# A decoder layer with a mixture of experts: the products into the experts as three f16 products, the expert's weights read in place, eight row buffers

## The chip, the cores and the metric

The kernel runs on one core of a Trainium2 chip. The metric is the device time of one execution in microseconds (us); lower is better. TensorE (PE) multiplies matrices, VectorE (DVE), ScalarE (ACT) and GpSimd (POOL) work elementwise, and SyncE (SP) issues transfers. "PEld" is the loading of a product's stationary operand (its weights) into PE; a "q" behind an engine's name means its sequencer, which runs register and issue instructions.

## The reference

One decoder layer over x, 128 batches of 64 rows of 128 numbers, thus 8192 tokens, or 64 tiles of 128. Three blocks follow each other, each added to its input and normalised: attention with retention ("ret"), attention over ctx_1024 ("cross"), and causal self attention ("self") with a mixture of 8 experts. The change touches the experts:

```python
probs = jax.nn.softmax(h @ wg, axis=-1)
topv, topi = jax.lax.top_k(probs, K)                 # K = 2 of E = 8
...
h1 = jax.nn.gelu(jnp.einsum('bsd,edf->ebsf', h, w1) + bb1[:, None, None, :])
y = jnp.einsum('ebsf,efd->ebsd', h1, w2) + bb2[:, None, None, :]
moe = jnp.einsum('ebsd,bse->bsd', y, w)
```

w1[e] is 128x512, w2[e] 512x128, all in float32.

## The kernel before, in words

**Attention.** The 192 tiles of the three blocks (64 each) go in 48 groups of four through a hand-written software pipeline. `sp_slot`, `pe_slot`, `act_slot`, `pool_slot` and `dve_slot` append to each engine's queue what it does in slot s, four slots to a group; every engine runs its queue in order and waits on semaphores. During the self groups a router picks two experts for each token, and POOL scatters the token's row (128 numbers, its number and its first choice) with an indirect DMA (L787) to `block_rows` in DRAM, a region for each expert.

**Weights.** `mixture` (L297) is a list of constants that SP loads one a slot in the cross phase, among them all experts' matrices and biases into one tile `wx` (L140), 1156 numbers an expert and partition: w1, w2, the 4 columns of bb1 and a row of bb2.

**The expert stage.** A block is 128 rows of one expert; there are NBLK = 135 of them. Which expert and which rows a block has is only known at run time: small tables `row_of` and `expert_of` are computed first for 73 early blocks and then, during the stage, for the rest. The loop at L1274 issues slot s: on SP `sp_expert` (L1181) reads a row number from the table into a register and loads `xrow` from `block_rows` at that address (L1188, L1189), at most four blocks ahead. DVE reads the expert's number (L1232) and copies its 1156 columns of `wx` to one of four buffers `we` (L1236). PE transposes the rows (L1194), ACT copies them to `hTb` (L1218). Four products of 128x128x128 (L1202) give the hidden layer, transposed, ACT adds bb1 and applies gelu (L1225), four products that accumulate (L1211) give the output, DVE adds bb2 (L1242), works out the row numbers (L1248), and POOL scatters 128 rows to `expert_rows` in DRAM (L1254). In slot s each engine takes the blocks in this order: out(s-3), transpose(s), in(s-1). Every third slot, for the first 54, also appends one slot of the tail of attention (`behind`). From slot 59 on, every fourth slot SP loads a piece of `x2b` (L1262).

The order on PE, which stays the same around the change (from L1274 on):

```python
if s >= 3:
    pe_expert_out(s - 3)
    dve_expert_out(s - 3)
...
if s < NBLK:
    sp_expert(s)
    pe_expert_turn(s)
    act_expert_turned(s)
if 1 <= s <= NBLK:
    pe_expert_in(s - 1)
    act_expert(s - 1)
```

A combine stage then weighs the two results of each token, normalises twice and stores.

## Time and profile before

| | us |
|---|---|
| median of 3 runs | 1290.16 |
| lowest, highest | 1288.4, 1293.84 |
| the profiled execution's own time | 1299.05 |
| its span | 1297.8 |
| first row load of the experts issued | 858.2 |
| last block's scatter issued | 1208.2 |

The mean granted clock of TensorE in the profiled execution is 0.893 of full speed. A page of the profile gives busy times over the whole span; views give the same for a stretch ("windows"), single instructions in order of time ("timeline"), all instructions of a source line with shortest, median and longest duration, who waited for whom ("waits"), and the chain of work that ended last.
### The profile page before, as it was taken

The numbers are of one execution on the slowest core, as the hardware profiler recorded it, in microseconds if no ns is written. First come the engines' busy times: TensorE is split into PE (matmuls) and PEld (weight loads), VectorE is DVE, ScalarE is ACT, GpSimd is POOL, SyncE is SP. The second block draws the span as 40 slices with busy tenths as digits, with TensorE's granted clock in tenths as the row PEclk, the third lists the DMA queues.
The fourth block names the chain that finished last, engine by engine and source line by source line (L and its number), as shares of the span: only waits on it lengthen the run. The fifth ranks groups of instructions, "written<-read, shape, count | busy, mean of one in ns | idle before, by whom it ended". The sixth has DMA issues, their size and how long they took to land.

```text
span 1297.8 us, 45997 instructions
## 1 busy us (share of the span) xinstructions
PE 1063.3 (82%) x17677; PEld 761.5 (59%) x17677; DVE 865.0 (67%) x2370; ACT 824.6 (64%) x1884; POOL 911.1 (70%) x859
## 2 busy tenths in 40 slices
PE   5888888788998888888988888847788799999552
PEld 2555555554555555555555555637777789999310
DVE  4677776766888777777767776545454466666485
ACT  2355554678999887777777776414445466666377
POOL 3788888866766657777777776766666656667596
PEclk9999898987999999989888997657889999999886
DMA  5465332221233223222222221111212233332453
GB/s 158 129 185 147 88 86 63 63 60 54 75 85 85 80 66 85 68 67 68 79 65 65 77 77 35 52 34 43 61 54 63 66 88 98 99 100 78 143 164 97
DMA packets 132181, 108.61 MB, mean 84 GB/s; under 512 B 19563, under 2 KB 122476, under 8 KB 131932
## 3 DMA queue, kind: packets, MB, share of 16 engines
q1 hardware_dynamic: 123548, 88.29, 24.9%
q0 software_dynamic: 8416, 17.38, 3.8%
q8 instruction: 141, 2.31, 0.8%
q14 instruction: 76, 0.62, 0.2%
HBM read 41.58 MB, written 26.75 MB: 53 GB/s over the span
## 4 chain that ended last, share of the span: by engine, by line
PE 42%; issue 14%; DVE 14%; POOL 14%; ACT 10%; DMA 3%; another core or an unknown queue 2%; DVEq 1%; SPq 1%; POOLq 0%; ACTq 0%
PE bank L1211 7%; PE bank L1202 7%; POOL Plo L769 7%; PE bank L547 3%; PE bank L612 3%; PE bank L550 3%; DVE P L841 2%; DMA xrow<-block_rows 2%; PE bank L487 2%; DVE st L873 2%; DVE mx L817 2%; PE bank L450 2%; PE bank L517 2%; PE bank L510 2%
## 5 line engine op out<-in xcount | busy, mean ns | idle before, releaser
L769 POOL TENSOR_TENSOR Plo<-P 128x1024 f16<-128x1024 f32 x192 | 364.7, 1901 | 162.2 <-ACT P L726 136.1
L1254 POOL DMA_INDIRECT expert_rows<-yo,ix x135 | 173.0, 1281 | 103.3 <-DVE ix L1248 73.4
L1225 ACT ACTIVATE G<-bank,we 128x128 f32<-128x128 f32 x540 | 154.9, 372 | 103.6 <-PE bank L1202 85.3
L817 DVE TENSOR_REDUCE mx<-bank 128x16 f16<-128x1024 f32 x128 | 156.7, 1225 | 42.3 <-PE bank L465 33.2
L687 ACT ACTIVATE Kz<-kh,col 128x512 f16<-128x512 f16 x256 | 167.1, 717 | 0.1
L1211 PE MATMUL bank<-we,G 128*128 128x128 f32 x1080 | 151.5, 286 | 16.7 <-ACT G L1225 12.6
L787 POOL DMA_INDIRECT block_rows<-xs,slots x128 | 132.6, 1036 | 39.8 <-issue 38.4
L510 PE MATMUL bank<-Vh,P 64*128 64x17 f16 (+1 forms) x3072 | 148.6, 170 | 10.2 <-issue 10.2
L726 ACT ACTIVATE P<-bank 128x1024 f32<-128x1024 f32 x128 | 131.1, 1024 | 39.7 <-PE bank L487 38.2
L510 PEld LDWEIGHTS bank<-Vh,P 64*128 64x128 bf16 x3072 | 125.6, 94 | 49.8 <-issue 37.2
L511 PE MATMUL bank<-Vh,Plo 64*128 64x17 f16 (+1 forms) x3072 | 145.9, 168 | 9.4 <-issue 9.3
L1202 PE MATMUL bank<-hTb,we 128*128 128x128 f32 x1080 | 149.1, 283 | 4.6 <-issue 4.4
L512 PE MATMUL bank<-Vl,P 64*128 64x16 f16 x3072 | 146.3, 167 | 7.4 <-issue 7.3
L1211 PEld LDWEIGHTS bank<-we,G 128*128 128x128 f32 x1080 | 138.1, 200 | 19.2 <-ACT G L1225 14.5
L1236 DVE COPY we<-wx 128x1156 f32 x135 | 104.4, 774 | 57.4 <-issue 54.1
L1202 PEld LDWEIGHTS bank<-hTb,we 128*128 128x128 f32 x1080 | 137.3, 199 | 5.6 <-issue 4.9
L512 PEld LDWEIGHTS bank<-Vl,P 64*128 64x128 bf16 x3072 | 127.4, 94 | 11.7 <-issue 11.6
L511 PEld LDWEIGHTS bank<-Vh,Plo 64*128 64x128 f16 x3072 | 127.9, 95 | 9.2 <-issue 9.2
L487 PEld LDWEIGHTS bank<-Qz,Kst 64*64 64x64 f16 x3072 | 60.8, 114 | 88.1 <-issue 62.1
L487 PE MATMUL bank<-Qz,Kst 64*64 64x128 f16 x3072 | 85.1, 233 | 28.2 <-DVE P L841 25.9
L732 ACT ACTIVATE xs<-xs,nmr,rstd 128x128 f32<-128x128 f32 x192 | 79.0, 488 | 17.0 <-POOL nmr L780 17.0
L443 PE MATMUL bank<-W,ident 128*128 128x256 f32 (+1 forms) x192 | 84.8, 527 | 3.0 <-DVE Vl L835 2.7
(187 smaller groups left out, 2169.5 us busy)
## 6 DMA issues: line engine op xcount, KB each, us to landing
Qz<-qh SPq DMA_DIRECT2D x192, 64.0 KB, 2.0
Kst<-kh SPq DMA_DIRECT2D x192, 64.0 KB
xrow<-block_rows SPq DMA_DIRECT2D x135, 65.0 KB
y_t<-expert_rows SPq DMA_DIRECT2D x16, 512.0 KB, 4.1
Qz<-ql SPq DMA_DIRECT2D x96, 64.0 KB, 2.0
Kst<-kl SPq DMA_DIRECT2D x96, 64.0 KB
xT<-xt SPq DMA_DIRECT2D x16, 256.0 KB, 3.1
xs<-x SPq DMA_DIRECT2D x16, 256.0 KB, 4.1
```

The lines of the kernel that those rows point to most:

```text
L487: i = pe.matmul(bank[64 * b:64 * b + 64, T_BANK + r, j * P:(j + 1) * P], Kst[g % 2][64 * r:64 * r + 64, j, at:at + S], Qz[g % 2][64 * r:64 ...
L510: pe.matmul(o, up[rows_b, cs], Vh[g % 3][rows_b, t, c, 0:nv], start=True, stop=False)
L511: pe.matmul(o, lo[rows_b, cs], Vh[g % 3][rows_b, t, c, 0:nv], start=False, stop=False)
L512: i = pe.matmul(o[:, 0:2 * DH], up[rows_b, cs], Vl[g % 3][rows_b, t, c, :], start=False, stop=True)
L687: i = act.activation(Kz[g % 2][:, slot, :], kh[g % 2][:, :], ACT.Identity, scale=column(f"slot{slot}"))
L769: pool.tensor_tensor(Plo[n % 3][:, :], P32[n % 3][:, :], upper(n), ALU.subtract).then_inc(f_Pl.of(n), 1)
L787: pool.indirect_dma_start(buf[:, :], bass.IndirectOffsetOnAxis(slots[i % 2][:, u:u + 1], 0), xs[:, i * GT + t, :], None).then_inc(l_rows.o ...
L817: dve.tensor_reduce(columns, bank[:, S_BANK:S_BANK + 2, :].rearrange("p r (j i k) -> p r j i k", i=2, k=S), AX_X, ALU.max, negate=True).th ...
L1202: i = pe.matmul(bank[:, 2 + p, c * P:(c + 1) * P], we[b][:, W1 + c * P:W1 + (c + 1) * P], hTb[p][:, :], start=True, stop=True)
L1211: i = pe.matmul(bank[:, 4 + p, 0:P], G[b][:, c, :], we[b][:, W2 + c * P:W2 + (c + 1) * P], start=c == 0, stop=c == FC - 1)
L1225: i = act.activation(G[b][:, c, :], bank[:, 2 + p, c * P:(c + 1) * P], ACT.Gelu_apprx_tanh, bias=we[b][:, B1 + c:B1 + c + 1])
L1254: pool.indirect_dma_start(ydst[:, :], bass.IndirectOffsetOnAxis(ix2[s % 4][:, :], 0), yo[s % 4][:, :], None).then_inc(b_sc.of(s), 16)
```

## The change

The matrices into the experts, w1, are kept as two f16 halves, high and low (`wx1`), and those out, w2, as float32 (`wx2`). w1 is loaded during the self groups into attention's five gate buffers; ACT rounds each expert's matrix to f16 (the high half), POOL subtracts that from it (the low half). In the expert stage DVE's copy of an expert's weights is gone: PE reads the expert's number into a register of its own and takes the weights in `wx1` and `wx2` at that register's address. The transposed rows are split the same way (ACT: `xhi`, DVE: `xlo`), and each product in is three f16 products, high by high, low rows by high weights, high rows by low weights, into one float32 sum. The biases come by a DMA for each block, which SP issues at a second register's address, into one of eight buffers `eb`. Row buffers `xrow` are eight instead of four. The core of the diff:

```diff
-    WW = 2 * F_N + FC + P
-    W1, W2, B1, B2 = 0, F_N, 2 * F_N, 2 * F_N + FC
+    HIGH, LOW = 0, 1
     buf = nc.dram_tensor("block_rows", ((E_N * REGION + 1 + SPARE) * P, RW), F32).ap()
     ydst = nc.dram_tensor("expert_rows", (TRASH + 2 * T_N, P), F32).ap()

-    wx = sb("wx", [P, E_N, WW])
+    wx1 = sb("wx1", [P, E_N, 2, F_N], F16)
+    wx2 = sb("wx2", [P, E_N, F_N])
...
+    CHUNKS = E_N
+    w_ld = count("w_ld", 16, len(gate))
+    w_high, w_low = count("w_high"), count("w_low")
+    LOADED, HIGHS, LOWS = {}, {}, {}
+    for j in range(0, CHUNKS, 2):
+        g = AT["self", 1] + j
+        for c in range(2):
+            LOADED.setdefault(GT * (g - 1), []).append(j + c)
+            HIGHS[GT * g + c] = j + c
+        LOWS[GT * (g + 1) + 3] = j
+        LOWS[GT * (g + 2) + 1] = j + 1
+
+    def expert_part(j, part):
+        return wx1[:, j, part, :]
+
+    def sp_expert_weights(j):
+        sp.wait_ge(*f_OTg(NG - 1))
+        sp.wait_ge(*w_low(j - len(gate)))
+        sp.dma_start(gate[j % len(gate)][:, :], w1[j]).then_inc(w_ld.of(j), 16)
+
+    def act_expert_weights(j):
+        act.wait_ge(*w_ld(j))
+        act.copy(expert_part(j, HIGH), gate[j % len(gate)][:, :]).then_inc(w_high.of(j), 1)
+
+    def pool_expert_weights(j):
+        pool.wait_ge(*w_high(j))
+        pool.tensor_tensor(expert_part(j, LOW), gate[j % len(gate)][:, :], expert_part(j, HIGH), ALU.subtract).then_inc(w_low.of(j), 1)
...
-        xrow = [sb(f"xrow{p}", [P, RW]) for p in range(4)]
+        AHEAD = 8
+        xrow = [sb(f"xrow{p}", [P, RW]) for p in range(AHEAD)]
         ix2 = [sb(f"ix2_{p}", [P, 1], U32) for p in range(4)]
-        hTb = [sb(f"hTb{p}", [P, P]) for p in range(2)]
-        we = [sb(f"we{p}", [P, WW]) for p in range(4)]
-        G = [sb(f"G{p}", [P, FC, P]) for p in range(4)]
+        xhi, xlo = ([sb(f"{n}{p}", [P, P], F16) for p in range(2)] for n in ("xhi", "xlo"))
+        eb = [sb(f"eb{p}", [P, FC + P]) for p in range(AHEAD)]
...
         pe.wait_ge(s_table[0], TABLE_DONE[0])
+        pe.wait_ge(*w_low(CHUNKS - 1))
...
         def sp_expert(s):
             if s == EARLY_BLOCKS:
                 sp.wait_ge(s_table[1], TABLE_DONE[1])
                 for i in range(NG - 2, NG):
                     sp.wait_ge(*l_rows(i))
-            sp.wait_ge(*b_xT(s - 4))
-            sp.wait_ge(*b_ix(s - 4))
+            sp.wait_ge(*b_xT(s - AHEAD))
+            sp.wait_ge(*b_ix(s - AHEAD))
             first = sp.value_load(row_of[0:1, order[s]:order[s] + 1], min_val=0, max_val=(E_N * REGION + SPARE) * P)
-            sp.dma_start(xrow[s % 4][:, :], buf[bass.ds(first, P), :]).then_inc(b_ld.of(s), 16)
+            sp.dma_start(xrow[s % AHEAD][:, :], buf[bass.ds(first, P), :]).then_inc(b_ld.of(s), 16)
+            sp.wait_ge(*b_g(s - AHEAD))
+            sp.wait_ge(*b_yo(s - AHEAD))
+            e = sp.value_load(expert_of[0:1, order[s]:order[s] + 1], min_val=0, max_val=E_N - 1)
+            sp.dma_start(eb[s % AHEAD][:, :], biases[bass.ds(e, 1), :, :].rearrange("o p w -> (o p) w")).then_inc(b_eb.of(s), 16)
+
+        def pe_expert_of(s):
+            if s == EARLY_BLOCKS:
+                pe.wait_ge(s_table[1], TABLE_DONE[1])
+            chosen_of[s] = pe.value_load(expert_of[0:1, order[s]:order[s] + 1], min_val=0, max_val=E_N - 1)

         def pe_expert_turn(s):
             pe.wait_ge(*b_ld(s))
-            pe.wait_ge(*b_xTs(s - 2))
-            pe.transpose(bank[:, s % 2, 0:P], xrow[s % 4][:, 0:P], ident[:, :]).then_inc(b_xT.of(s), 1)
+            pe.wait_ge(*b_xlo(s - 2))
+            pe.transpose(bank[:, s % 2, 0:P], xrow[s % AHEAD][:, 0:P], ident[:, :]).then_inc(b_xT.of(s), 1)
+
+        def first_weights(s, part, c):
+            return wx1[:, bass.ds(chosen_of[s], 1), part, c * P:(c + 1) * P].rearrange("p o w -> p (o w)")
+
+        def second_weights(s, c):
+            return wx2[:, bass.ds(chosen_of[s], 1), c * P:(c + 1) * P].rearrange("p o w -> p (o w)")

         def pe_expert_in(s):
-            p, b = s % 2, s % 4
-            pe.wait_ge(*b_xTs(s))
-            pe.wait_ge(*b_we(s))
+            p = s % 2
+            pe.wait_ge(*b_xlo(s))
             pe.wait_ge(*b_g(s - 2))
             for c in range(FC):
-                i = pe.matmul(bank[:, 2 + p, c * P:(c + 1) * P], we[b][:, W1 + c * P:W1 + (c + 1) * P],
-                              hTb[p][:, :], start=True, stop=True)
+                o = bank[:, 2 + p, c * P:(c + 1) * P]
+                pe.matmul(o, first_weights(s, HIGH, c), xhi[p][:, :], start=True, stop=False)
+                pe.matmul(o, first_weights(s, HIGH, c), xlo[p][:, :], start=False, stop=False)
+                i = pe.matmul(o, first_weights(s, LOW, c), xhi[p][:, :], start=False, stop=True)
             i.then_inc(b_z.of(s), 1)

         def pe_expert_out(s):
...
             pe.wait_ge(*b_g(s))
             pe.wait_ge(*b_yo(s - 2))
             for c in range(FC):
-                i = pe.matmul(bank[:, 4 + p, 0:P], G[b][:, c, :], we[b][:, W2 + c * P:W2 + (c + 1) * P],
-                              start=c == 0, stop=c == FC - 1)
+                i = pe.matmul(bank[:, 4 + p, 0:P], G[b][:, c * P:(c + 1) * P], second_weights(s, c), start=c == 0, stop=c == FC - 1)
             i.then_inc(b_y.of(s), 1)
+            del chosen_of[s]

         def act_expert_turned(s):
             act.wait_ge(*b_z(s - 2))
             act.wait_ge(*b_xT(s))
-            act.copy(hTb[s % 2][:, :], bank[:, s % 2, 0:P]).then_inc(b_xTs.of(s), 1)
+            act.copy(xhi[s % 2][:, :], bank[:, s % 2, 0:P]).then_inc(b_xhi.of(s), 1)
+
+        def dve_expert_turned(s):
+            dve.wait_ge(*b_z(s - 2))
+            dve.wait_ge(*b_xhi(s))
+            dve.tensor_tensor(xlo[s % 2][:, :], bank[:, s % 2, 0:P], xhi[s % 2][:, :], ALU.subtract).then_inc(b_xlo.of(s), 1)
...
             act.wait_ge(*b_y(s - 4))
+            act.wait_ge(*b_eb(s))
...
-        def dve_expert_weights(s):
-            if s == EARLY_BLOCKS:
-                dve.wait_ge(s_table[1], TABLE_DONE[1])
-            e = dve.value_load(expert_of[0:1, order[s]:order[s] + 1], min_val=0, max_val=E_N - 1)
-            dve.wait_ge(*b_yo(s - 4))
-            dve.wait_ge(*b_y(s - 4))
-            dve.wait_ge(*b_g(s - 4))
-            dve.tensor_copy(we[s % 4][:, :], wx[:, bass.ds(e, 1), :].rearrange("p o w -> p (o w)")).then_inc(b_we.of(s), 1)
...
             dve.wait_ge(*b_sc(s - 4))
+            dve.wait_ge(*b_eb(s))
             dve.wait_ge(*b_y(s))
-            dve.tensor_tensor(yo[b][:, :], bank[:, 4 + p, 0:P], we[b][:, B2:B2 + P], ALU.add).then_inc(b_yo.of(s), 1)
+            dve.tensor_tensor(yo[b][:, :], bank[:, 4 + p, 0:P], eb[s % AHEAD][:, FC:], ALU.add).then_inc(b_yo.of(s), 1)
...
-            if s < NBLK:
-                dve_expert_weights(s)
...
                 sp_expert(s)
+                pe_expert_of(s)
                 pe_expert_turn(s)
                 act_expert_turned(s)
+                dve_expert_turned(s)
```

In `mixture` the entries for w1, bb1 and bb2 are gone, and `biases` is an input laid out as 8 x 128 x 132. The loads of `x2b` use the semaphores of the rows' loads.

## Rows read from the trace of the kernel before

**Rows 1.** The page, its part 1, busy time of TensorE

```profile
PE 1063.3 (82%) x17677; PEld 761.5 (59%) x17677; DVE 865.0 (67%) x2370; ACT 824.6 (64%) x1884; POOL 911.1 (70%) x859
```

**Rows 2.** Windows: length; PE, PEld, DVE, ACT, POOL busy (count); clock, DMA share, GB/s

```profile
450.00:620.00 170.00, 149.47 (x3082) 95.89 (x3083) 127.12 (x346) 128.30 (x205) 117.98 (x108) 0.90 0.25 70
...
879.00:1045.00 166.00, 133.58 (x1032) 127.80 (x1032) 79.70 (x249) 80.78 (x290) 103.25 (x94) 0.91 0.20 58
1045.00:1207.00 162.00, 155.79 (x1365) 152.44 (x1363) 106.60 (x258) 106.34 (x399) 111.08 (x81) 1.00 0.32 93
1207.00:1298.00 91.00, 39.25 (x65) 12.82 (x64) 59.28 (x344) 54.79 (x150) 65.43 (x89) 0.76 0.46 140
```

**Rows 3.** The chain of waits from 879 to 1207 us, its shares by line

```profile
by line: PE bank L1211 28.7%; PE bank L1202 28.6%; DMA xrow<-block_rows 8.7%; issue 5.8%; another core or an unknown queue 5.2%; PE bank L1194 5.2%; ACT G L1225 5.2%; DVE we L1236 2.1%; DVEq L1232 2.1%; SPq L1188 1.8%; PE bank L580 1.3%; DV
```

**Rows 4.** Timeline of PE, one late block: start us, us, line, operation

```profile
1120.50 0.27 PE L1194 MATMUL bank<-ident,xrow 128*128 128x128 f32 x1
1120.61 1.06 PE L1202 MATMUL bank<-hTb,we 128*128 128x128 f32 x8
1121.51 1.06 PE L1211 MATMUL bank<-we,G 128*128 128x128 f32 x8
1122.40 0.27 PE L1194 MATMUL bank<-ident,xrow 128*128 128x128 f32 x1
```

**Rows 5.** Waits from 1045 to 1207 us, the transposes' own

```profile
PEld bank L1194 <- DMA xrow<-block_rows: 6.9, 10, 1.2
```

**Rows 6.** SP: timeline at 858, its lines' durations (min/median/max), its wait late

```profile
858.17 2.76 SPq L1189 DMA_DIRECT2D xrow<-block_rows  x3
...
L1188 SPq TENSOR_LOAD <-row_of x135: 17/268/487, 857.1 to 1198.7; - x135
L1188 SPq FUSED_REGOPS  x135: 17/152/705, 857.7 to 1199.0; - x135
...
L1189 SPq FUSED_REGOPS  x135: 3/42/648, 858.0 to 1199.3; - x135
...
L1189 SPq DMA_DIRECT2D xrow<-block_rows x135: 3/338/721, 858.2 to 1199.4; - x135
...
L1262 SPq DMA_DIRECT2D x2b<-x_scratch x16: 7/438/446, 1046.5 to 1168.6; - x16
...
SPq L1187 <- DVE ix L1248: 54.6, 67, 1.6
```

**Rows 7.** PE in attention: scores, sums (first and last of 48 pairs), router

```profile
642.08 0.39 PE L487 MATMUL bank<-Qz,Kst 64*64 64x128 f16 x16
...
L487 PE MATMUL bank<-Qz,Kst x3072: 212/216/313, 27.5 to 856.8; 64*64 64x128 f16 x192
...
642.40 0.19 PE L510 MATMUL bank<-Vh,P 64*128 64x17 f16 x2
...
643.00 0.18 PE L512 MATMUL bank<-Vl,P 64*128 64x16 f16 x2
...
487.77 0.32 PE L575 MATMUL bank<-chosen,onesb 128*128 128x56 bf16 x7
```

**Rows 8.** DVE's load of a register and the address of its copy

```profile
L1232 DVEq TENSOR_LOAD <-expert_of x135: 298/304/549, 876.7 to 1200.2; - x135
L1232 DVEq FUSED_REGOPS  x135: 190/190/206, 877.3 to 1200.5; - x135
...
L1236 DVEq FUSED_REGOPS  x135: 57/57/65, 877.7 to 1200.9; - x135
```

**Rows 9.** The bias addition on DVE and the scatter on POOL

```profile
L1242 DVE TENSOR_TENSOR yo<-bank,we x135: 270/292/293, 889.0 to 1207.2; 128x128 f32<-128x128 f32 x135
...
L1254 POOL DMA_INDIRECT expert_rows<-yo,ix x135: 956/1367/1529, 890.0 to 1208.2; - x135
```

**Rows 10.** ACT and POOL on tiles of attention

```profile
L721 ACT COPY hT<-bank x16: 586/587/647, 452.1 to 959.4; 128x512 f32<-128x512 f32 x16
...
L769 POOL TENSOR_TENSOR Plo<-P x192: 1884/1895/2400, 29.6 to 862.2; 128x1024 f16<-128x1024 f32 x192
```

More of the change, by code:

```diff
@@ L103, in __call__, with build @@
         return self.sems[i % len(self.sems)], max(i // len(self.sems) + 1, 0) * self.inc
-def build(nc, x, xt, ctxt, wmats, cols, rows, const_ident, const_masks, const_ids, const_tri, const_experts, const_steps, const_blocks, const_region, const_pads, const_rows, wg, w1, bb1t, w2, bb2, out):
+def build(nc, x, xt, ctxt, wmats, cols, rows, const_ident, const_masks, const_ids, const_tri, const_experts, const_steps, const_blocks, const_region, const_pads, const_rows, wg, w1, w2, biases, out):
     T_N = x.shape[0] * x.shape[1]
@@ L435, in sp_slot @@
             sp_mixture(s - NG)
+        for j in LOADED.get(s, ()):
+            sp_expert_weights(j)
     def pe_keep_clock(o, times):
@@ L807, in pool_slot @@
             pool_dispatch(*PLACED[s])
+        if s in LOWS:
+            pool_expert_weights(LOWS[s])
     def dve_maxima(n):
@@ L1117, in moe_phase @@
         wb = sb("wb", [P, NT])
-        xrow = [sb(f"xrow{p}", [P, RW]) for p in range(4)]
+        AHEAD = 8
+        xrow = [sb(f"xrow{p}", [P, RW]) for p in range(AHEAD)]
         ix2 = [sb(f"ix2_{p}", [P, 1], U32) for p in range(4)]
-        hTb = [sb(f"hTb{p}", [P, P]) for p in range(2)]
-        we = [sb(f"we{p}", [P, WW]) for p in range(4)]
-        G = [sb(f"G{p}", [P, FC, P]) for p in range(4)]
+        xhi, xlo = ([sb(f"{n}{p}", [P, P], F16) for p in range(2)] for n in ("xhi", "xlo"))
+        eb = [sb(f"eb{p}", [P, FC + P]) for p in range(AHEAD)]
+        G = [sb(f"G{p}", [P, FC * P]) for p in range(4)]
         yo = [sb(f"yo{p}", [P, P]) for p in range(4)]
@@ L1175, in moe_phase @@
         order = [*range(EARLY_BLOCKS), *range(EARLY_BLOCKS + 1, NBLK, 2), *range(EARLY_BLOCKS, NBLK, 2)]
-        b_ld = count("b_ld", 16, 4)
-        b_xT, b_xTs, b_we, b_z, b_g, b_y, b_ix, b_yo = (count(n_) for n_ in
-                                                        ("b_xT", "b_xTs", "b_we", "b_z", "b_g", "b_y", "b_ix", "b_yo"))
+        b_ld, b_eb = (count(n_, 16, AHEAD) for n_ in ("b_ld", "b_eb"))
         b_sc = count("b_sc", 16, 4)
+        b_xT, b_xhi, b_xlo, b_z, b_g, b_y, b_ix, b_yo = (count(n_) for n_ in (
+            "b_xT", "b_xhi", "b_xlo", "b_z", "b_g", "b_y", "b_ix", "b_yo"))
+        chosen_of = {}
         def sp_expert(s):
@@ L1246, in dve_expert_rows @@
             dve.wait_ge(*b_sc(s - 4))
-            dve.tensor_scalar(ix2[s % 4][:, :], xrow[s % 4][:, P + 1:P + 2], code[:, order[s]:order[s] + 1], xrow[s % 4][:, P:P + 1],
+            dve.tensor_scalar(ix2[s % 4][:, :], xrow[s % AHEAD][:, P + 1:P + 2], code[:, order[s]:order[s] + 1], xrow[s % AHEAD][:, P:P + 1],
                                ALU.is_equal, ALU.add).then_inc(b_ix.of(s), 1)
@@ L1255, in pool_expert_out @@
                                     None).then_inc(b_sc.of(s), 16)
-        x_ld = count("x_ld", 16, NS)
         x_b = count("x_b")
         def sp_x(q):
-            sp.dma_start(x2b[:, q * MT:(q + 1) * MT, :], x_by_step[q]).then_inc(x_ld.of(q), 16)
+            sp.dma_start(x2b[:, q * MT:(q + 1) * MT, :], x_by_step[q]).then_inc(l_x.of(NG + q), 16)
         def dve_x(q):
             x_q = x2b[:, q * MT:(q + 1) * MT, :]
-            dve.wait_ge(*x_ld(q))
+            dve.wait_ge(*l_x(NG + q))
             dve.tensor_tensor(x_q, x_q, brow("b2"), ALU.add).then_inc(x_b.of(q), 1)
@@ L1483, in lay_out @@
     c = np.ascontiguousarray
+    biases = np.concatenate([N("bb1").reshape(E_N, FC, P).transpose(0, 2, 1),
+                             np.broadcast_to(N("bb2")[:, None, :], (E_N, P, P))], 2).astype(np.float32)
     def turned(v):
```

16 lines of the change are left out of this document (7 added, 9 removed).

## The prediction

> **What bounds the kernel now.** I read the page first: PE is busy 82% of the span [rows 1]. The change touches the expert stage, so I cut the span there by a view of windows [rows 2]. Start-up and the combine stage (from 1207) stay as they are. Between lie 166 us in which 55 blocks pass beside the tail of attention (the early part) and 162 us with 78 blocks alone (the late part): 3.0 and 2.08 us a block. PE is busy 133.6 of 166 and 155.8 of 162. In the chain through both parts the two products have 29% each, the xrow transfer 8.7%, the transposes 5% [rows 3].
>
> The timeline of PE shows one late block [rows 4]: transpose 0.11 us, four float32 products in (8 records, 0.90), four out (8 records, 0.89): 1.90 us with no gap. A float32 product is two records of 112 ns. The rest to 2.08 is waiting, mostly for xrow [rows 5].
>
> Then the queue that feeds PE. SP issued its first three row loads with nothing to wait for: three issues in 2.76 us, the last one's record 0.34, so (2.76 - 0.34)/2 = 1.21 us for one load at a register's address [rows 6]. Its large parts stand there: reading the register 0.27, address arithmetic 0.15 and 0.04, issue 0.34 = 0.80; two tiny instructions and the gaps make 1.21, a factor of 1.5, or some 0.06 an instruction. Today SP does one such load a block, and its queue waits 54.6 us of the late 162 for DVE: it has slack.
>
> **The change, part by part.** Durations are of the profiled execution, 1299.05 us (span 1297.8), 9 us over the median 1290.16; I carry differences from it to the median.
>
> 1. Products in: twelve f16 products for four float32 ones. The trace has no f16 product of 128x128 weights and 128 columns. Nearest: the scores' 16 f16 matmuls of 128 columns, four in the array at a time, end 0.39 us after they start, one lasting 0.216: three further rounds in 0.17, 58 ns each [rows 7]. The 128x128 weights in 16 bits that follow each other there, seven in 0.32 us with one lasting some 0.18, leave 24 ns for each, so weights are no bound. Twelve products take 12 x 0.058 = 0.70 us instead of 0.90. Bounds: 0.67 (a quarter of float32's 224 ns each) to 1.34 (112 ns each, no gain from f16). PE's engine goes from 1.90 to 1.70 us a block. That is all that the arithmetic gives: 0.20 x 133 = 27 us if PE stayed the bound.
>
> 2. PE's sequencer gets one register load a block and addresses at twelve distinct offsets from the register, in sixteen products. PE does none of this in the trace. DVE does: load 0.304, arithmetic 0.190, then 0.057 for the one address of its copy [rows 8]. Load: 0.49, with SP's factor 0.74. Addresses: 12 x 0.057 = 0.68 (repeated offsets reused, no gaps) to 16 x 0.057 x 1.5 = 1.37. Register work is 1.17 to 2.11 us a block. Its cost below: it all runs ahead of the engine, nothing. Above: none is hidden, 1.70 + 2.11 = 3.81 us a block. I take 2.11, nearest to DVE's and SP's rows with their gaps (the same operations on the same kind of sequencer), plus 42 matmul and weight instructions (attention's 48 pairs pass in 0.6 us, 6 ns each [rows 7]: 0.26) and three waits (0.06 each, 0.18): 2.55 us. Behind PE's load in order stand the transpose and the products of three blocks; ACT and DVE wait for those.
>
> 3. SP now also issues a bias load at a register's address for every block, the same sequence with the same two waits: 2 x 1.21 = 2.42 us a block. The 16 loads of x2b (0.44 each, 0.5 with the gap [rows 6]) add 8 us: 2.52 in the late part. That is over today's 2.08, and eight buffers do not help a queue that issues too slowly; they give a lead of about five blocks (b_g and b_yo of block s-8 come three slots behind), 12 us once.
>
> By itself: the Trainium skill ("DMA: Bandwidth & Descriptors", Issuing engines are not separate DMA queues) calls a sequencer's time to initiate a DMA usually small beside the DMA, and its anatomy table gives some 50 ns for the dispatch. By that the pair would be near 0.1 us and SP no bound, as in Rival B; the rows above are 24 times that.
>
> 4. Eight row buffers. The waits for xrow, about 7 us in the late part [rows 5] and, by the chain, more early, go as far as SP keeps up.
>
> 5. DVE loses the copy of the weights and its load, and gains a 128x128 subtraction of some 0.29 [rows 9]; it is busy 1.37 us a late block today, ACT 1.36 [rows 2]. POOL's scatters have a median of 1.37 and a shortest of 0.96 [rows 9]. All lie under 2 us, beside a longer period: I cost them at nothing; the cover is SP's 2.4 us, and without it POOL with its gaps comes next, at 1.9. The subtraction is one more link between transpose and product, but the product comes a slot later, 2 us, which covers 0.29.
>
> 6. In attention: eight loads of 256 KB, eight ACT conversions of 128x512 (0.59 by the copy of that size, 4.7 in all), eight POOL subtractions (half of 1.90, 7.6 in all) [rows 10]. Of 170 us there ACT is busy 128, POOL 118, PE 149 [rows 2]. Between 0 and 12 us; I take 2, since most slots have room. SP issues them two at a time, 0.9 us by x2b's row, in every second group of some 18 us (858 us for 48): nothing.
>
> **The sum.** Early, 55 blocks. Today: 55 x 1.90 = 105 of engine time, 29 of other PE work (133.6 - 105), 32 idle. After: 55 x 2.55 + 29 + 20 (the slower pace covers part of the old idle time) = 189, +23. Late: PE's 2.55 and SP's 2.52 nearly coincide: 78 x 2.55 = 199, +37. With part 6: +62. So 1299 + 62 = 1361 for a profiled run, **1352** against the median. Its own range, 2.3 to 2.8 us a block: 1324 to 1385.
>
> **Rivals.**
>
> Rival A, SP alone binds; PE's register work runs ahead. For it: products follow each other without gaps today, so PE's queue is filled early [rows 4]. Against: 2.11 exceeds 1.70. Early: 55 x 1.70 + 29 + 27 = 150, -16; SP needs 133 and keeps up. Late: 197 - 12 of lead = 185, +23. With 2: 1290 + 9 = 1299, about no change.
>
> Rival B, the faster side: the place is SP's pair of loads. If a pair costs less than 2.08 us, today's late period, the kernel gains; for that the second load must overlap the first's issue. For it: some issue records are far shorter (minimum 3 ns [rows 6]). Against: the median is 0.338, the same as in the three free loads. Then PE sets 1.70: late 133, -29; early -16; with 2: 1290 - 43 = 1247.
>
> Rival C, little is hidden on PE: at 3.81 us a block early 55 x 3.81 + 61 = 271, +105; late 297, +135; 1532. Halfway, at 3.18, about 1440. For it: waits and registers share one queue in order, and an engine with gaps may lose its clock: in the tail, where PE is busy 39 of 91 us, the granted clock is 0.76, against 1.00 in the late part [rows 2]. At the lower level, 1.2 GHz, the engine part doubles to 3.4.
>
> By itself: the Trainium skill ("TensorE: Matmul & The Clock Gate", Wait — 56ns, not 53.3ns?) says that with hardware decoding off the sequencer's microcode spends about 62 ns on a MATMUL. The 6 ns an instruction in attention say that it isn't off here; whether an address in a register brings the microcode back no row shows. Twenty such instructions would be 1.24 us more, an estimate by that page, and the time would be near 1500.
>
> Rival D, the change doesn't do what it says: f16 brings nothing (112 ns a product), PE's engine takes 2.34 us. Under 2.55 that stays hidden: at most +8 us over the forecast.
>
> **How the numbers follow.** The forecast 0.50, A 0.15, B 0.17, C 0.13, D 0.05. A measurement of this kernel can tell some 0.5%, 6.5 us, from no change. Faster: B and a little of A, 0.19. Within 0.5%: half of A, 0.08. Slower: the rest, 0.73. The range, 1275 to 1440, leaves out most of B (0.12) and the worse part of C (0.08).
>
> **What would show it.** The late part takes 185 to 215 us for 78 blocks. SP's timeline shows two issues a block some 1.2 us apart, and its waits for DVE are gone. PE's idle time there is put down to "issue" or to the transfers of xrow or eb, with 40 us or more in place of 6, and PE's busy share falls below 80%. Twelve f16 records take 0.7 us where they follow without gaps. I am wrong if the late period is under 2.08 us, or if SP's pair costs less than 2.0. If the late part is over 240 us, it is Rival C.

## The result, and the profile after

The changed kernel takes **1354.63 us** (median of 4 runs, 1351.28 to 1358.66) against 1289.28 (4 runs, 1282.47 to 1293.84): a ratio of 1.0513, 95% interval 1.0457 to 1.0569. The profiled run took 1358.66 us (span 1357.4). Run again later, on another chip, it came to a ratio of 1.0481 [1.0412, 1.0551]. The forecast was 1352, so the sum came out. Its terms did not all, and in the run on the other chip two of them are different.

First the same cuts as in [rows 2]: windows of the changed kernel (length; busy time and count of PE, PEld, DVE, ACT, POOL; clock, DMA share, GB/s). The lines are attention in two pieces, the early part and the late part.

```profile
450.00:620.00 170.00, 136.12 (x2672) 85.50 (x2675) 126.09 (x293) 115.66 (x188) 111.03 (x99) 0.83 0.23 65
620.00:879.00 259.00, 224.56 (x4321) 142.07 (x4321) 181.02 (x495) 167.33 (x267) 177.69 (x161) 0.76 0.21 60
901.00:1062.00 161.00, 151.66 (x1260) 123.60 (x1260) 56.48 (x258) 84.58 (x294) 92.81 (x101) 0.91 0.36 90
1062.00:1261.00 199.00, 195.28 (x1631) 150.37 (x1630) 68.96 (x251) 108.61 (x387) 79.90 (x77) 1.00 0.36 97
```

The late part is 199 us where it was 162. In the first 170 us of these windows PE has 2672 matmuls behind it, in [rows 2] it had 3082: attention, which the change hardly touches, runs late. To put both on one scale I take four marks from each trace, the starts of the transposes of the first block, of block 57 and of the last block, and the end:

| us | first block | block 57 | last block | end | median late period |
|---|---|---|---|---|---|
| before | 874.6 | 1045.8 | 1201.7 | 1297.8 | 1.90 |
| after | 900.9 | 1062.2 | 1260.7 | 1357.4 | 2.574 |
| difference of the stage | +26.3 | -9.9 | +42.6 | +0.6 | |

So of 59.6 us, attention lost 26.3, the early part gained 9.9 and the late part lost 42.6. The late part takes 198.4 to 198.8 us in every later run that keeps the addresses; the other two numbers do not hold, as a later section shows.

PE's timeline shows a late block, beside [rows 4] (start us, us, line, operation):

```profile
1150.19 0.23 PE L1250 MATMUL bank<-xhi,wx 128*128 128x128 f16 x1
1150.25 0.22 PE L1251 MATMUL bank<-xlo,wx 128*128 128x128 f16 x1
1150.31 0.23 PE L1252 MATMUL bank<-xhi,wx 128*128 128x128 f16 x1
1150.44 0.23 PE L1250 MATMUL bank<-xhi,wx 128*128 128x128 f16 x1
...
1151.32 1.15 PE L1260 MATMUL bank<-wx,G 128*128 x8
1152.50 0.30 PE L1236 MATMUL bank<-ident,xrow 128*128 128x128 f32 x1
1152.72 0.23 PE L1250 MATMUL bank<-xhi,wx 128*128 128x128 f16 x1
```

Read the starts, not the durations: these records overlap. Three products of a group start 0.06 us apart, but the next group starts 0.25 after the last. Products in take 1.13 us of the block (1150.19 to 1151.32) where they took 0.90, products out 1.18 (0.89), the transpose 0.22 (0.11). The busy share can't show this: the records of PE cover 195 of 199 us, because each is longer than the step to the next. What held PE up stands in its queue (durations min/median/max in ns):

```profile
L1231 PEldq TENSOR_LOAD <-expert_of x135: 296/301/503, 900.0 to 1260.0; - x135
L1231 PEldq FUSED_REGOPS  x135: 151/151/165, 900.5 to 1260.3; - x135
...
L1250 PEldq FUSED_REGOPS  x540: 46/46/51, 903.3 to 1263.5; - x180
L1250 PEld LDWEIGHTS bank<-xhi,wx x540: 95/96/151, 903.4 to 1263.6; 128*128 x180
```

One register load a block, 0.45 us in its two large records, and 540 address computations on each of L1250 and L1260, four a block; those for the low weights (L1252) make twelve. The second product of a group (L1251) uses the first one's address again. The single records of one block's pass through this queue, ahead of the transpose at 1152.50 (count, ns, first to last start in us):

```profile
L1250 PEldq FUSED_REGOPS  x4: 46/46/46, 1150.1 to 1150.9; - x4
L1252 PEldq FUSED_REGOPS  x4: 46/46/46, 1150.2 to 1151.0; - x4
L1260 PEldq FUSED_REGOPS  x4: 46/46/46, 1151.2 to 1151.6; - x4
L1231 PEldq TENSOR_LOAD <-expert_of x1: 305/305/305, 1151.7 to 1151.7; - x1
L1235 PEldq EVENT_SEMAPHORE  x1: 51/51/51, 1152.4 to 1152.4; - x1
```

Taken over the late part (medians), the queue goes from one address to the next in 0.124 us, which the starts above show too (1150.19, 1150.31, 1150.44). Twelve of these steps are 1.49 us, with the issue of the products in them. The register load keeps the queue 0.65 us from its start to the next wait, and three waits take 0.34. Together that is 2.47 of the 2.574 us; the rest is in a few longer steps.

SP's timeline, then its waits in the late part (us in total, times, longest):

```profile
1149.99 0.34 SPq L1222 DMA_DIRECT2D xrow<-block_rows  x1
1151.18 0.34 SPq L1226 DMA_DIRECT2D eb<-biases  x1
1152.34 0.34 SPq L1222 DMA_DIRECT2D xrow<-block_rows  x1
```
```profile
SPq L1224 <- DVE yo L1289: 3.0, 11, 0.6
SPq L1221 <- PE bank L1236: 3.0, 9, 0.5
```

A pair of loads costs 2.35 us. SP's waits have fallen from 54.6 us [rows 6] to 6.3. Both queues are nearly full, and the waits of the other engines (late part) show which one the blocks hang on:

```profile
DVE yo L1289 <- PE bank L1260: 115.4, 77, 2.4
...
PEld bank L1236 <- issue: 14.5, 74, 0.3
```

Nobody waits for a transfer; PE waits for its own issue.

### The profile page after: what moved, and what is told of

Its sections match the earlier page's. It is cut to its first block, busy times and chain, and to the rows that moved or that the text cites. A ratio compares the mean times of both kernels' runs of the same rounds, so it can differ in the third digit from the quotient of the medians.

```text
span 1357.4 us, 49537 instructions
## 1 busy us (share of the span) xinstructions
PE 1142.9 (84%) x18217; PEld 767.4 (57%) x18217; DVE 822.7 (61%) x2370; ACT 835.2 (62%) x1892; POOL 875.8 (65%) x867
## 4 chain that ended last, share of the span: by engine, by line
PE 38%; POOL 27%; issue 19%; ACT 7%; DVE 7%; DMA 1%; POOLq 0%; ACTq 0%; SPq 0%; DVEq 0%
POOL Plo L797 15%; PE bank L1260 12%; PE bank L1250 5%; POOL block_rows L815 3%; PE bank L1252 3%; PE bank L1236 3%; PE bank L1251 2%; DVE P L871 2%; POOL rstd L806 2%; PE bank L573 2%; PE bank L576 2%; PE bank L638 1%; DVE st L903 1%; ACT Kz L713 1%; ACT O L894 1%
## 5 line engine op out<-in xcount | busy, mean ns | idle before, releaser
L1301 POOL DMA_INDIRECT expert_rows<-yo,ix x135 | 135.4, 1003 | 178.4 <-DVE ix L1295 165.0
L1280 ACT ACTIVATE G<-bank,eb 128x128 f32<-128x128 f32 x540 | 154.0, 368 | 109.0 <-PE bank L1252 108.2
L847 DVE TENSOR_REDUCE mx<-bank 128x16 f16<-128x1024 f32 x128 | 156.8, 1225 | 45.1 <-PE bank L491 44.5
L1260 PE MATMUL bank<-wx,G 128*128 x1080 | 160.4, 293 | 1.4 <-issue 0.5
L1289 DVE TENSOR_TENSOR yo<-bank,eb 128x128 f32<-128x128 f32 x135 | 39.4, 292 | 197.1 <-PE bank L1260 197.0
L536 PE MATMUL bank<-Vh,P 64*128 64x17 f16 (+1 forms) x3072 | 140.5, 170 | 9.4 <-POOL Plo L797 6.7
L1260 PEld LDWEIGHTS bank<-wx,G 128*128 128x128 f32 x1080 | 135.7, 197 | 17.5 <-issue 2.8
L537 PE MATMUL bank<-Vh,Plo 64*128 64x17 f16 (+1 forms) x3072 | 137.9, 168 | 0.1
L538 PE MATMUL bank<-Vl,P 64*128 64x16 f16 x3072 | 137.6, 167 | 0.0
L1250 PE MATMUL bank<-xhi,wx 128*128 128x128 f16 x540 | 123.0, 230 | 1.7 <-DVE xlo L1272 1.2
L1252 PE MATMUL bank<-xhi,wx 128*128 128x128 f16 x540 | 123.0, 230 | 0.0
L1251 PE MATMUL bank<-xlo,wx 128*128 128x128 f16 x540 | 118.9, 223 | 0.0
```

The source lines that it names most:

```text
L536: pe.matmul(o, up[rows_b, cs], Vh[g % 3][rows_b, t, c, 0:nv], start=True, stop=False)
L537: pe.matmul(o, lo[rows_b, cs], Vh[g % 3][rows_b, t, c, 0:nv], start=False, stop=False)
L538: i = pe.matmul(o[:, 0:2 * DH], up[rows_b, cs], Vl[g % 3][rows_b, t, c, :], start=False, stop=True)
L847: dve.tensor_reduce(columns, bank[:, S_BANK:S_BANK + 2, :].rearrange("p r (j i k) -> p r j i k", i=2, k=S), AX_X, ALU.max, negate=True).th ...
L1250: pe.matmul(o, first_weights(s, HIGH, c), xhi[p][:, :], start=True, stop=False)
L1252: i = pe.matmul(o, first_weights(s, LOW, c), xhi[p][:, :], start=False, stop=True)
```

## Which queue sets the late period

Theory: PE's sequencer at some 2.55 us a block, SP's at 2.5 right behind. Rivals: SP alone, or the f16 products themselves. Four kernels undo one or both, each run once, on one chip, where the kernel before took 1293.5 us (one run); a fifth asks for the share of the second products alone.

**One row load a block on SP.** The bias load is made for the first eight blocks only:

```diff
-            e = sp.value_load(expert_of[0:1, order[s]:order[s] + 1], min_val=0, max_val=E_N - 1)
-            sp.dma_start(eb[s % AHEAD][:, :], biases[bass.ds(e, 1), :, :].rearrange("o p w -> (o p) w")).then_inc(b_eb.of(s), 16)
+            if s < AHEAD:
+                sp.dma_start(eb[s][:, :], biases[s:s + 1, :, :].rearrange("o p w -> (o p) w")).then_inc(b_eb.of(s), 16)
```

> The changed kernel, but the bias buffers are loaded once for the first eight blocks and used again for all later ones (so most blocks get another expert's biases); SP issues one load a block. In the changed kernel every block from about 955 to 1261 us takes 2.57 us, early and late alike, and SP waits only 6.3 us of 203. Theory PE (PE's sequencer, with its register load and twelve address computations a block, sets the period, SP's 2.52 us being just under it): the period stays 2.50 to 2.57 and the time falls by under 10 us from 1355; SP's queue waits for 90 us or more of the late part. Theory SP (its pair of loads sets the period): the period falls to 2.0 or less and the time by 60 us or more.

Measured: 1357.55 us, late period 2.574 as before. SP now has time to spare:

```profile
SPq L1220 <- DVE ix L1293: 93.7, 70, 2.2
```

**Fixed weights on PE.** SP keeps its pair; PE's register load is gone and every address is expert 0's:

```diff
-            chosen_of[s] = pe.value_load(expert_of[0:1, order[s]:order[s] + 1], min_val=0, max_val=E_N - 1)
-        return wx1[:, bass.ds(chosen_of[s], 1), part, c * P:(c + 1) * P].rearrange("p o w -> p (o w)")
+        return wx1[:, 0:1, part, c * P:(c + 1) * P].rearrange("p o w -> p (o w)")
```

> The changed kernel, but PE takes expert 0's weights at a fixed address for every block: no register load and no address computations on PE; SP keeps both loads. Theory PE with SP just behind: the period falls only to SP's 2.42 to 2.52 us, 2 to 12 us less in all, and PE now waits for the transfers of rows and biases. Theory SP: no change (within 3 us). If SP's pair costs nothing where PE is fast: a period of 1.7 to 2.0 us and 80 us less.

Measured: 1326.68 us, mean late period 2.527. The bound has passed from PE's queue to SP's: in the waits of the late part PE now stands for the rows. The time fell by some 30 us, not by 2 to 12. Only 4 of them are in the late part (194.6 us for 198.5), as expected; most are in the early part, 137.8 us where the changed kernel took 161.3 and the run with one row load 156.7.

```profile
PEld bank L1235 <- DMA xrow<-block_rows: 52.7, 50, 2.7
```

**Neither.** Both edits at once.

> Both edits together: one load a block on SP and fixed weights on PE. Both theories: the engine itself sets the period, 0.11 for the transpose, 0.70 in, 0.89 out, 1.70 us, if POOL's scatter (1.0 with 0.3 between) and ACT (1.4) fit beside it. The late part falls from 201 to 133 to 150 us, the early part to 140 to 155, the time to about 1275 to 1290 with the slower attention of the changed kernel left in. If neither sequencer is the cause, nothing changes.

Measured: 1257.73 us, mean late period 1.739, nearly every interval 1.73. The early part took 131.0 us (140 to 155 expected), and the time is below the 1275 to 1290 expected. Its timeline of PE shows what the f16 products are worth when nothing holds them:

```profile
1100.10 0.27 PE L1233 MATMUL bank<-ident,xrow 128*128 128x128 f32 x1
1100.20 0.22 PE L1247 MATMUL bank<-xhi,wx 128*128 128x128 f16 x1
1100.26 0.22 PE L1248 MATMUL bank<-xlo,wx 128*128 128x128 f16 x1
1100.32 0.22 PE L1249 MATMUL bank<-xhi,wx 128*128 128x128 f16 x1
...
1100.88 1.11 PE L1257 MATMUL bank<-wx,G 128*128 128x128 f32 x8
1101.82 0.27 PE L1233 MATMUL bank<-ident,xrow 128*128 128x128 f32 x1
```

Twelve products from 1100.20 to 1100.88: 0.68 us, 57 ns each, and no gap between groups. Out 0.94, transpose 0.10.

**The register load kept, the addresses fixed.** As "neither", but PE reads its register and doesn't use it.

> As the run with one load on SP and fixed weights, but PE still loads the expert's number to a register once a block and doesn't use it. It tells what of PE's sequencer time is the load and what the addresses. If the load (0.68 us from its start to the next instruction in the trace of the changed kernel) runs beside the engine's 1.70 us: within 0.05 us a block of the run without it. If it drains the queue: 0.2 to 0.5 us a block more, 25 to 65 us in all, and the addresses are the smaller part of the loss.

Measured: 1258.67 us, period 1.739, the same. The load is hidden here, where no address is added to it.

**Addresses for the products out alone.** One row load, fixed weights for the products in:

```diff
-        return wx1[:, bass.ds(chosen_of[s], 1), part, c * P:(c + 1) * P].rearrange("p o w -> p (o w)")
+        return wx1[:, 0:1, part, c * P:(c + 1) * P].rearrange("p o w -> p (o w)")
```

> The changed kernel with one row load a block on SyncE (biases of the first eight experts only) and fixed addresses for the products into the experts; the register load and the four addresses of the products out of them stay. If each address costs 0.07 us of the sequencer whatever stands before it, the late period is 1.74 + 4 * 0.07 = 2.02 us and the time about 1279. If addresses ahead of the float32 products hide behind them (each of these takes 0.22 us of the engine), the period stays at 1.74 us and the time at about 1258.

Measured: late period 1.772 (median; mean 1.844, with one pair of intervals of 5.09 and 2.48), most intervals 1.75 to 1.82. Neither number expected: four addresses added 0.05, not 0.28 and not nothing. The time, 1303.39 us, was far above both expectations, for a reason outside the late part: it ran on another chip (the kernel before 1308.08 us there), and its early part took 179.8 us where that of "neither" took 131.0 (next section).

What follows. With no address the period is 1.73 and nearly constant, the engine's. With four it is 1.77 and uneven, with twelve 2.574. Eight more addresses cost (2.574 - 1.772)/8 = **0.10 us each**. That is the least they can cost, since the sequencer with four may still be under the engine's time; the trace of the changed kernel has a step of 0.124 us for an address with the products that follow it. If the kernel with four is just at the edge, its sequencer needs 1.77 us a block, and so 1.37 without any address, register load included; that lies under 1.73, and the load is hidden. This last split is worked out, not measured by itself. It fits that even the products out grew from 0.94 to 1.18 us in the changed kernel: their eight records start within 0.88 us (1151.32 to 1152.20), and the next transpose, at 1152.50, stands behind the register load. A queue that is the bound has no lead, so its 0.65 us for the load are not hidden there.

## Where attention's 26 us came from, and where they went

In the changed kernel nine of the 16 executions of VectorE's L921, and some of L923, were slow; in the kernel before the same line (L891) took 660 to 686 ns each time. Line L921 of the changed kernel (ns, min/median/max):

```profile
L921 DVE TENSOR_TENSOR xs<-xs,row x16: 660/1295/5624, 449.6 to 963.8; 128x512 f32<-128x512 f32 x16
```

DVE's and POOL's timelines at the slowest one:

```profile
524.59 0.69 DVE L865 TENSOR_TENSOR Vl<-bank,Vh 128x512 f16<-128x512 f32 x1
525.20 5.62 DVE L921 TENSOR_TENSOR xs<-xs,row 128x512 f32<-128x512 f32 x1
```
```profile
523.57 3.75 POOL L797 TENSOR_TENSOR Plo<-P 128x1024 f16<-128x1024 f32 x2
527.28 1.15 POOL L410 TENSOR_TENSOR wx<-gate,wx 128x512 f16<-128x512 f32 x1
528.38 1.88 POOL L797 TENSOR_TENSOR Plo<-P 128x1024 f16<-128x1024 f32 x1
```

POOL works without a break from 523.57 to 530.26, the added subtraction (L410) among it, and VectorE's operation ends 0.56 us after that, about its own 0.66. Line L865, as wide, but with one input in PSUM, ran beside the same POOL instructions in its usual 0.69. That is the rule of the Trainium skill ("SBUF — State Buffer", SBUF: two separate sides): a VectorE operation with two SBUF inputs and a GpSimd operation that reads SBUF take a shared port pair in turn, the whole instruction long. The trace agrees, and shows more: on this stretch the operation did not get in between POOL's instructions, so it waited for the whole chain. Behind it stood VectorE's maximum (L847), for which PE waited 26.7 us from 575 to 780 (8.1 before, 560 to 740; 11.0 in the second run of the same kernel, below), and the granted clock of 620 to 879 was 0.76, against 0.81 before (620 to 874).

Theory: the added conversion of the weights makes this. Three kernels try it.

**No conversion.** Constants of the halves' size come by DMA straight to the f16 weights; ACT's and POOL's instructions are left out.

```diff
-        if s in HIGHS:
-            act_expert_weights(HIGHS[s])
-        if s in LOWS:
-            pool_expert_weights(LOWS[s])
```

> The changed kernel without the conversion in attention: the eight loads bring constants of the same size straight to the f16 weights, ACT and POOL convert nothing (the experts' first matrices are then constants, and one more input exists). In the changed kernel attention ends 26 us later than before (first transpose of the experts at 900.9 us, not 874.6), though the sixteen added instructions last 14 us in all and end at 540 us; DVE's multiplications of 128x512 by g1 rose from 0.68 us to 1.3 to 5.6 us in eight groups, the pair of multiplication and addition from 22 to 43.5 us in sum. Theory collision (POOL's added subtractions shift its queue, so that DVE's two-input operations now meet POOL's long ones and wait): first transpose back at 873 to 882, the sum back at 22 to 25, the time 20 to 27 us less. Theory own time (the added instructions and transfers cost what they last): 5 to 14 us less. Theory layout (the shorter list of constants, other addresses): no change.

**The kernel before, with the conversion** in the same slots, its result unused.

> The kernel before, with the change's loads and conversions added in attention (to three spare tiles that nobody reads) and nothing else of the change. Theory collision: first transpose 18 to 28 us later than 874.6, the multiplications by g1 slow in several groups, the time 18 to 28 us more. Theory own time: 5 to 14 us more. Theory layout: 0 to 3 us more.

**The conversion earlier**, ahead of the groups with the slow operations:

```diff
-        g = AT["self", 1] + j
+        g = AT["self", 0] - 2 + j // 2
-        LOWS[GT * (g + 1) + 3] = j
-        LOWS[GT * (g + 2) + 1] = j + 1
+            LOWS[GT * g + 2 + c] = j + c
```

> The changed kernel with the conversions in the four groups before the router starts, two a group, done by about 400 us; the first multiplication by g1 comes at 449 us. Theory collision: POOL's queue is as before by then: first transpose at 875 to 886, the sum of the pair 22 to 27, the time 14 to 26 us less than the changed kernel, about 1330 to 1340. If the shift persists whatever its place: 0 to 5 us less.

| us | first block | early part | late part | end | L921 and L923 in all |
|---|---|---|---|---|---|
| after | 900.9 | 161.3 | 198.5 | 1357.4 | 43.5 |
| no conversion | 875.8 | 190.3 | 198.4 | 1361.0 | 24.0 |
| conversion earlier | 879.9 | 185.1 | 198.8 | 1360.3 | 23.9 |
| before with conversion | 881.1 | 170.6 | 158.6 | 1306.2 | 25.2 |
| before | 874.6 | 171.2 | 155.9 | 1297.8 | 22.0 |

By itself this looked like a proof: without the conversion, or with it elsewhere, attention ends on time. But the total did not move (1362.72 us; 1366.08 median, ratio 1.0482 [1.0396, 1.0568]), since the early part grew by as much, and in the kernel before with the conversion attention ended 6.5 us later, not 18 to 28. Its time, 1307.50 us (one run), is that of the kernel before on the same chip, 1307.43. The forecast of 14 to 28 us in the time failed in all three. They ran on a chip where the kernel before took 1307.43 us and not 1289. So I ran the changed kernel again, as it is, on a third chip (before: 1308.08).

> The changed kernel once more, on the same chip as its version with the conversion moved. If the place of the conversion is worth nothing in total, the ratio is 1.045 to 1.055 as in its first measurement, attention ends at about 901 us and the early part takes about 161 us with TensorE idle under 12 us of it. If the longer early part of the two runs without the collision (185 and 190 us) belonged to the chip they ran on, this run shows a longer early part too where it runs on a chip with a slower kernel before.

Measured: ratio 1.0481 [1.0412, 1.0551], first block at **879.7**, early part **186.9**, late part 198.6, end 1361.7. Same code, no collision to speak of, the long early part. Its slowest L921, and POOL beside it:

```profile
523.04 1.92 DVE L921 TENSOR_TENSOR xs<-xs,row 128x512 f32<-128x512 f32 x1
```
```profile
519.56 3.75 POOL L797 TENSOR_TENSOR Plo<-P 128x1024 f16<-128x1024 f32 x2
523.26 1.15 POOL L410 TENSOR_TENSOR wx<-gate,wx 128x512 f16<-128x512 f32 x1
525.50 1.95 POOL L797 TENSOR_TENSOR Plo<-P 128x1024 f16<-128x1024 f32 x1 [1.09 <-ACT P L752]
```

Here the operation begins as POOL's pair ends, and POOL then waits 1.09 us for its input: VectorE gets in. What differs is where in POOL's pair it starts: 1.63 us after the pair's start in the first run, 3.48 in this one. Whether that is the chip's doing I can only say so far: the four kernels of the first comparison, on one chip, all showed the 5.6 us and ended attention at 895.6 to 904.4, and the three with the conversion in its old place on the third chip (this one, the one with addresses for the products out alone, and one of the next section) showed at most 1.9 us in this line and ended it at 879.7 to 889.8. So no run took the conversion out where the collision was seen. That the conversion makes it there is argued and not shown, and the kernel before has no trace from that chip. The place of the conversion made no difference that was measured: 1.0482 there, 1.0481 here.

**What stays open** is the early part, 161 us in the one case and 185 to 190 in the other. The waits of ACT in it (us in total, times, longest), of the changed kernel's second run and then of its first:

```profile
ACT xhi L1267 <- PE bank L1236: 49.9, 24, 14.6
ACT G L1280 <- remote: 31.6, 8, 4.5
```
```profile
ACT G L1280 <- PE bank L1252: 42.3, 53, 1.1
ACT xhi L1267 <- PE bank L1236: 36.7, 53, 6.5
```

Eight stalls of some 4 us are put down to an unknown releaser. In them ACT stands still for 3.8 to 4.7 us and VectorE for 2.6 to 4.5, and they start again within 0.3 us of each other; PE works on for a part of it. SP goes through its queue in steps of 0.7 or 1.4 us, and its records, 0.34 us for an issue otherwise, shrink to 3 to 30 ns at times. The issues of `eb` in the early part (ns, min/median/max), in the second run and in the first:

```profile
L1226 SPq DMA_DIRECT2D eb<-biases x56: 3/338/727, 879.8 to 1066.6; - x56
```
```profile
L1226 SPq DMA_DIRECT2D eb<-biases x58: 337/338/765, 902.5 to 1060.9; - x58
```

Issues under 30 ns are a mark that sorts the traces. The changed kernel's first trace and the four kernels of the first comparison have none of some 1000, and no wait over 2 us of ACT or VectorE in the early part is put down to "remote". All eight traces from the other two chips have 16 to 34 of them and 9 to 21 such waits. So does the trace of the kernel before from which the differences above are taken (13 and 10). It is of the other kind than the changed kernel's first trace, and the +26.3 and -9.9 compare two kinds. Its like is the second run: there attention is +5.1, the early part +15.7 and the late part +42.6. The instruction transfers are as many and as long in both kinds (14 on each of two queues in the early part). I found no cause; whether it is the chip, and why the collision comes only with traces that have no such stalls, no run told apart.

## What would beat both

**The kernel before with eight row buffers** (and nothing else):

```diff
-        xrow = [sb(f"xrow{p}", [P, RW]) for p in range(4)]
+        xrow = [sb(f"xrow{p}", [P, RW]) for p in range(8)]
-            sp.wait_ge(*b_xT(s - 4))
-            sp.wait_ge(*b_ix(s - 4))
+            sp.wait_ge(*b_xT(s - 8))
+            sp.wait_ge(*b_ix(s - 8))
```

> The kernel before with eight row buffers in place of four and nothing else. The waits for rows, 6.9 us late, and the gaps that follow them (every fourth or so block takes 2.5 to 3 us, not 1.90) should go: late period 2.02 to 1.90 to 1.95, 5 to 10 us less there, 0 to 6 us early: the time 5 to 15 us less. If POOL's scatter (1.52 with 0.38 between, 1.90) is what paces the late part, the same period of 1.90 and the same gain. If the scatters' landing (the waits of DVE for them) ends the waits, under 3 us.

Measured: 1294.49 us (10 runs) against 1307.43 on the same chip, **0.9899 [0.9866, 0.9932]**. Late part 147.7 us instead of 155.9, early part the same. Its wait list for PE in the late part has a single entry; before, the transposes alone waited 6.9 us for rows [rows 5]. The time, 12.9 us less, is within the 5 to 15 expected.

```profile
PE bank L1211 <- issue: 0.2, 1, 0.2
```

**f16 products, weights still copied.** Added to that: the f16 halves lie in the expert's row of `wx`, VectorE copies all 1156 columns to a fixed buffer as it did, and PE has no register. Twelve f16 products go in:

```diff
+                parts = we[b][:, W1:W1 + F_N].bitcast(F16)
+                high, low = (parts[:, h * F_N + c * P:h * F_N + (c + 1) * P] for h in (HIGH, LOW))
+                pe.matmul(o, high, xhi[p][:, :], start=True, stop=False)
+                pe.matmul(o, high, xlo[p][:, :], start=False, stop=False)
+                i = pe.matmul(o, low, xhi[p][:, :], start=False, stop=True)
```

> The kernel before with eight row buffers and with the products into the experts as three f16 products, but with VectorE still copying each expert's rows (the f16 halves, the float32 weights out of it and both biases, 1156 columns as before) into a buffer at a fixed address; nothing on TensorE and only one load on SyncE at a register's address. The theory that the change loses by TensorE's address computations and SyncE's second load, and not by the f16 products, expects a late period between 1.74 (the run without either) and 1.90 us (the kernel before), with VectorE's chain of about 1.8 us a block the likely bound (register load 0.3 and 0.15, copy 0.76, three small operations of 0.2), so 0 to 12 us less over the late part, and attention ending 5 to 26 us later than before: a ratio to the kernel before between 0.98 and 1.01. The rival, that f16 products themselves cost more than they save, expects a late period of 2.0 us or more and a ratio above 1.02.

> The same kernel with the conversion of the weights moved ahead of the groups in which VectorE's additions were slow. If the conversion's place costs what it cost in the changed kernel and the rest doesn't give it back here, attention ends within 6 us of the kernel before (874 to 881 us) and the ratio is 0.97 to 0.99, 10 to 20 us below the run with the old place. If the early part gives everything back, as it did in the changed kernel, the two are within 0.4%.

Measured: 1304.26 us, 0.9982 [0.9948, 1.0016], and with the conversion earlier 1304.91, 0.997 [0.9928, 1.0012]; by the intervals neither differs from the kernel before. So neither beats it: what eight row buffers alone gain (0.9899, on another chip) is not there, with a late part of 153.4 us for 147.7. The late period has 1.73 us as its commonest value, the engine's, but a mean of 1.99, over the 1.74 to 1.90 expected and just at the rival's 2.0; the ratio is not over 1.02, as the rival has it. The late part's windows and waits name the next bound:

```profile
1066.00:1220.00 154.00, 142.94 (x1637) 131.63 (x1636) 114.55 (x331) 101.59 (x388) 89.63 (x78) 1.00 0.33 92
```
```profile
PEld bank L1240 <- DVE xlo L1262: 16.4, 38, 1.0
```

VectorE carries the copy (0.76), three small operations and a queue with its own register load, and every fourth block also an addition of 128x512 (0.69). PE waits for its low half of the input. The f16 products save 0.17 us a block only if somebody other than VectorE, SP or PE pays for choosing the expert. Of the moved conversion: the first block came at 877.5 instead of 889.8, but the 889.8 is from an execution of 1317.0 us, the slowest of its ten; in the medians the move was worth nothing, which is the 0.4% expected, not the 10 to 20 us.

## Why the prediction was right, and where only its sum was

- **PE's sequencer as the bound: right.** 2.574 us a block for 2.55. Removing its register work took the period to SP's, removing both to 1.739. This is what carries the forecast: +42.6 of the 59.6 us.
- **Its make-up: near.** I had 12 addresses for 1.37 us with gaps, load 0.74, instructions and waits 0.44. In the trace: load 0.65, twelve steps of 0.124 with the instructions in them 1.49 (for 1.37 and 0.26), three waits 0.34 (for 0.18).
- **f16 products: right.** 0.70 forecast, 0.68 measured; the bound 1.34 (Rival D) is out.
- **SP's pair: right.** 2.42, with x2b's loads 2.52; measured 2.35, and 2.527 where SP alone binds. Rival B, a pair under 2.08 us, goes with that. (The Trainium skill, "DMA: Bandwidth & Descriptors", Issuing engines are not separate DMA queues, calls a sequencer's time to initiate a DMA usually small relative to the DMA; the trace disagrees for a load at a register's address, with 1.2 us from one issue to the next and 2.0 us from issue to landing. The 50 ns that the prediction takes from an anatomy table of that page stand there for the path of a DMA that GpSimd issues, and these are SP's.) Rival A failed on its own condition: register work does not run ahead once it is over the engine's 1.70.
- **The late part: +37 forecast, +42.6 measured** (the kernel before passed it in 2.02 us a block, not the 2.08 of my window, and the period was 0.02 over). Within 185 to 215.
- **Attention: the step that failed in the first run.** Part 6 bounded it by 0 and 12 us, by slots with room on each engine, and took 2. It was +26.3 in the profiled run. Counting busy time per engine missed that two engines with room can still exclude each other; there 0.68 us became 5.62. In the second run, the nearer comparison, it was +5.1, within the bounds, and no run shows that the conversion made the rest.
- **The early part: +23 forecast, -9.9 and +15.7 measured** (186.9 against 171.2). The step that failed is that the sum laid 29 us of other work on PE and 20 us of idle time on top of 55 x 2.55. In the first trace the intervals have a median of 2.59 us with the tail of attention between the blocks, and 57 x 2.574 = 147 leaves 15 us of 161.3: the tail's products ran beside the sequencer's work. In the second run 40 us are left, and the waits put down to "remote" stand in them.
- **The total: right in the first run by luck as well.** These two errors have opposite signs: 26.3 - 9.9 = 16.4 where 2 + 23 = 25 stood. In the second run the terms are +5, +16 and +43 for +2, +23 and +37, against a profile of the kernel before from another chip. One sum of the prediction is off: from 2.55 down to 2.3 us a block is 133 x 0.25 = 33 us, so the range's own lower end is 1319 and not 1324.
- **The waits for rows: right** that they go, as part 4 says; that part alone is worth 1%, by the run with eight buffers.
- **POOL at no cost: right, with a gain unnamed.** Its scatter fell from a median of 1367 ns [rows 9] to 957. VectorE's copy no longer stands beside it: before, the 114 scatters that overlap a copy have a median of 1504 ns and the 21 others 962.

```profile
L1301 POOL DMA_INDIRECT expert_rows<-yo,ix x135: 952/957/1462, 914.8 to 1267.7; - x135
```

- **PE's busy share below 80%, 40 us of idle time: wrong.** It is 98%, with 14.5 us put to issue. A late load of weights stretches nothing that a busy count sees, since a record of 0.22 us covers the step of 0.12 to the next. The spacing of the starts is the reading to take.

## What to carry to other kernels

An operand at a register's address costs PE's sequencer 0.10 to 0.12 us for each distinct address, and the register load ahead of it 0.65. Count these per block beside the engine's own time: under it they are nearly free, over it they are the period, and many short products (twelve of 57 ns) are where it turns. Where a copy is replaced by addressing, ask which sequencer inherits the choice, and count every load at a register's address (1.2 us on SP) too. And before stage times of two kernels are compared, run the same kernel on two chips, and look for a mark of the execution in both traces (here SP's issue records): 21 to 26 us moved from one stage to another with no line changed.

## What the runs showed of the hardware that I had not expected

- A VectorE operation of 128x512 with both inputs in SBUF took 0.66 to 5.62 us, by where in POOL's chain it began; one with an input in PSUM, beside the same chain, always 0.69.
- Scatters on POOL took 0.96 us alone and 1.50 beside VectorE's copy of 128x1156 (medians of 21 and 114). With the copy kept beside f16 products the median was 1115 ns.
- The same kernel on two chips: attention's end 900.9 and 879.7 us, the early part 161.3 and 186.9, the whole 1357.4 and 1361.7. The second trace has SP issue records of 3 to 30 ns and stalls of some 4 us, the first has neither.
- A register load that takes 0.65 us of PE's queue costs nothing (1.739 with and without) while the queue's total is under the engine's.
- A product at a new register address came 0.124 us after the last such; a product that repeats the address has no computation and follows in 0.06.
